# Local attention on one core: the inverse norms ahead of the rotation sum on GpSimd, the cosine product later on VectorE, the feed-forward part in 12 slots of 16

## What is computed

```
qkv = shift_tokens(x) @ Wqkv                        # 16 heads of 64
q = l2norm(q) * qs;  k = l2norm(k) * ksc
q = q * cos * scale + rotate_half(q) * sin * scale
k = k * cos / scale + rotate_half(k) * sin / scale
out = local_attention(q, k, v)                      # windows of 32, each sees itself and the one before
x = x + out @ Wo
x = x + (a * gelu(gate)) @ W2 + b2                  # a, gate from layernorm(x) @ W1 + b1, inner width 341
```

## Time and profile before

| | |
|---|---|
| median of three runs | 5737.72 us (5737.62 to 5739.98) |
| the profiled execution's own time | 5798.86 us |
| its span | 5797.1 us |
| TensorE matmuls busy | 5247.6 us, 91% |
| VectorE busy | 4111.8 us, 71% |
| ScalarE busy | 3595.0 us, 62% |
| GpSimd busy | 3474.3 us, 60% |
| mean granted TensorE clock | 0.927 of full speed |

### The profile page before, as it was taken

The page is one execution under the profiler, slowest core; times in us unless marked ns, Lnnn a source line. Parts: engine busy times, 40 slices in busy tenths (PEclk is TensorE's granted clock), DMA queues, the critical chain, the costliest instruction groups (busy, mean ns, idle before and its releaser), DMA issues. The chain is left out here.

```text
span 5797.1 us, 142985 instructions
## 1 busy us (share of the span) xinstructions
PE 5247.6 (91%) x46548; PEld 3130.0 (54%) x46548; DVE 4111.8 (71%) x8327; ACT 3595.0 (62%) x10714; POOL 3474.3 (60%) x3696
## 2 busy tenths in 40 slices
PE   7999999999999985899999999899999999999997
PEld 4666566565666652333433433566656666565664
DVE  5888888888888862344434443688888888888885
ACT  4887778777787760022222222587777877777775
POOL 6888778777877751000000000788777777787784
PEclk8999999999999995588977897899999999999998
DMA  2121121212112111000000000212121121211211
GB/s 71 45 58 45 50 50 42 55 45 52 48 42 55 45 31 21 0 1 1 1 1 1 1 1 1 70 44 57 44 53 48 42 56 44 52 49 45 52 45 31
DMA packets 297778, 216.57 MB, mean 37 GB/s; under 512 B 83197, under 2 KB 294681, under 8 KB 296217
## 3 DMA queue, kind: packets, MB, share of 16 engines
q1 hardware_dynamic: 296984, 206.69, 14.1%
HBM read 41.87 MB, written 1.05 MB: 7 GB/s over the span
## 5 line engine op out<-in xcount | busy, mean ns | idle before, releaser
L742 ACT ACTIVATE prob<-ps,nmx,inv 128x96 f32<-128x96 f32 x3072 | 1284.1, 430 | 309.6 <-PE ps L673 266.1
L545 POOL TENSOR_TENSOR rot<-t 128x512 f32<-128x512 f32 x768 | 1026.8, 1337 | 714.8 <-DVE t L820 661.7
L549 POOL TENSOR_TENSOR inv<-ssm,neg_half 128x8 f32<-128x8 f32 x768 | 1415.7, 1843 | 0.0
L828 DVE TENSOR_TENSOR prob<-prob,rec 128x384 f32<-128x384 f32 x768 | 912.8, 1189 | 26.2
L627 PE MATMUL ps<-w_qkv,xs 128*128 128x512 f32 x1536 | 877.4, 654 | 59.0 <-DVE t L820 39.5
L1287 ACT ACTIVATE ptl<-ps_l 128x1024 f32<-128x1024 f32 (+1 forms) x288 | 281.1, 976 | 967.3 <-PE ps_l L1162 733.4
L836 DVE TENSOR_REDUCE mx<-ps 128x4 f32<-128x384 f32 x768 | 424.1, 552 | 377.5 <-PE ps L654 374.8
L673 PE MATMUL ps<-ident,prob 128*96 128x128 f32 x3072 | 475.7, 278 | 214.1 <-DVE prob L828 213.2
L742 ACT ACTIVATION_READ_ACCUMULATOR prob<-ps,nmx,inv 128x1 f32 x3072 | 622.8, 203 | 0.0
L820 DVE TENSOR_TENSOR t<-ps,tab_s 128x256 f32<-128x256 f32 x1536 | 572.0, 414 | 0.0
L735 ACT COPY vt<-ps 128x256 f32<-128x256 f32 x768 | 285.3, 371 | 435.2 <-PE ps L665 424.2
(11 more groups left out here) (201 smaller groups left out, 8635.7 us busy)
## 6 DMA issues: line engine op xcount, KB each, us to landing
vs<-vt SPq DMA_DIRECT2D x768, 96.0 KB, 2.2
vs<-vt SPq DMA_DIRECT2D x768, 64.0 KB, 2.0
vs<-vt SPq DMA_DIRECT2D x768, 32.0 KB, 1.8
xs<-x_a SPq DMA_DIRECT2D x384, 32.0 KB, 1.9
w_qkv<-in_L_ffn_Wqkv SPq DMA_DIRECT2D x48, 256.0 KB, 3.8
w_qkv<-in_L_ffn_Wqkv SPq DMA_DIRECT2D x48, 128.0 KB, 3.4
w_o<-in_L_ffn_Wo SPq DMA_DIRECT2D x12, 512.0 KB, 4.1
w<-in_L_ffn_W SPq DMA_DIRECT2D x12, 341.0 KB
```

Source lines behind the costliest of these rows:

```text
L545: nc.gpsimd.tensor_tensor(rot[:, n % 4], t1[:, n % 2], t2[:, n % 2], ALU.add).then_inc(z["rotated"], 1)
L549: nc.gpsimd.tensor_tensor(inv[:, n % 4], ssm[:, n % 2], neg_half[:, 0:2 * HU], ALU.pow).then_inc(z["inv_ready"], 1)
L742: e = nc.scalar.activation(prob[:, n % 2, h, :], scores[:, h % 2, h // 2, :], ACT.Exp, scale=inv[:, n % 4, h:h + 1], bias=nmx[:, n % 2, h: ...
L828: nc.vector.tensor_tensor(prob[:, n % 2], prob[:, n % 2], rec[:, n % 2].unsqueeze(2).to_broadcast([P, HU, SKEYS]), ALU.mult).then_inc(z["w ...
```

## The change

The phases of the feed-forward part are drawn together from slots 0 to 15 into slots 0 to 11, and four slots of each sixteen have none. On TensorE the feed-forward product moves ahead of the turn of `prob`; on VectorE the feed-forward step moves ahead of the sum of squares; on ScalarE square, gate copy and shift move behind the copy of the output. On GpSimd the power (`inv`) and the carrying of keys move ahead of the rotation sum, and the sum is done in two halves, keys first, each with a semaphore of its own. On VectorE the sine products come first, and the cosine product moves behind `nmx`. TensorE's query-key product waits for `t1_ready` instead of `t2_ready`. SP loads the feed-forward weights four slots earlier. What is computed stays the same.

```diff
--- before.py
+++ after.py
@@ -64,14 +64,15 @@
 
 
 
-PHASE = dict(shift=0, mean=1, centre=1, square=2, var=2, eps=2, rstd=3, diag=3, spread=4, scale=4,
-             gate=(5, 7, 8), gate_copy=(6, 8, 9), gelu=11, up=(11, 12, 13), prod=(11, 12, 13), down=15, add=15)
+PHASE = dict(shift=0, mean=1, centre=1, square=1, var=2, eps=2, rstd=2, diag=2, spread=3, scale=3,
+             gate=(4, 5, 6), gate_copy=(4, 5, 6), gelu=7, up=(7, 8, 9), prod=(7, 8, 9), down=11, add=11)
+
 
 
 SEMAPHORES = (
     "const_in consts_ready x_in wq_in_0 wq_in_1 wq_in_2 wq_in_3 wv_in_0 wv_in_1 wv_in_2 wv_in_3 wo_in sc_in wf_in"
 
-    " xs_in_0 xs_in_1 tab_ready qk_ready squared summed clamped inv_ready t1_ready t2_ready rotated k_normed"
+    " xs_in_0 xs_in_1 tab_ready qk_ready squared summed clamped inv_ready t1_ready t2_ready rotated_k rotated_q k_normed"
     " tr_ready tr_read s_ready k_carried maxed negated exped recip_ready weighted pt_ready pt_read v_ready v_read"
     " v_strips_0 v_strips_1 v_strips_2 v_strips_3"
     " o_ready ot_read y_ready x_b_ready"
@@ -406,7 +407,7 @@
 
         def feed(j, part):
             g, p = divmod(j - LAG_Y, 16)
-            return (p, g - 1) if not (part == "first" and g < 1) else (None, None)
+            return (p, g - 1) if p <= 11 and not (part == "first" and g < 1) else (None, None)
 
         def group_no(L, g):
             return (L + L0) * G + g
@@ -420,7 +421,7 @@
             with eng.Fori(1, DEPTH) as L:
                 for j in range(UNITS):
                     slot(L, j, "steady")
-            for j in range(UNITS, UNITS + LAG_Y + 16):
+            for j in range(UNITS, UNITS + LAG_Y + 12):
                 slot(DEPTH - 1, j, "last")
 
         block = st.enter_context(nc.Block())
@@ -478,7 +479,7 @@
                         if j == LAG_Y:
                             sp.wait_ge(z["y_ready"], (L + L0) * TILES)
                             output_weights(L)
-                        if j == LAG_Y + 15:
+                        if j == LAG_Y + 11:
                             sp.wait_ge(z["x_a_ready"], (L + L0) * G + 1)
                             feed_forward_weights(L)
                     if j == UNITS - 6:
@@ -538,24 +539,28 @@
                     nc.gpsimd.tensor_tensor(f_rstd[:, :], f_var[:, :], neg_half[:, 0:GT // P], ALU.pow).then_inc(z["pow_ready"], 1)
                 if live(LAG_R):
                     n = (j - LAG_R) % 8
-                    pool.wait_ge(z["t1_ready"], done(LAG_R))
-                    pool.wait_ge(z["t2_ready"], 2 * done(LAG_R))
-                    if had(LAG_R, 4):
-                        pool.wait_ge(z["tr_ready"], done(LAG_R, 4))
-                    nc.gpsimd.tensor_tensor(rot[:, n % 4], t1[:, n % 2], t2[:, n % 2], ALU.add).then_inc(z["rotated"], 1)
                     pool.wait_ge(z["clamped"], done(LAG_R))
                     if had(LAG_R, 4):
                         pool.wait_ge(z["exped"], done(LAG_R, 4))
                     nc.gpsimd.tensor_tensor(inv[:, n % 4], ssm[:, n % 2], neg_half[:, 0:2 * HU], ALU.pow).then_inc(z["inv_ready"], 1)
-                    pool.wait_ge(z["rotated"], done(LAG_R))
-                    pool.wait_ge(z["inv_ready"], done(LAG_R))
-                    kh = rot[:, n % 4, QK // 2:QK].rearrange("p (h d) -> p h d", d=DH)
-                    nc.gpsimd.tensor_tensor(kh, kh, inv[:, n % 4, HU:2 * HU].unsqueeze(2).to_broadcast([P, HU, DH]), ALU.mult).then_inc(z["k_normed"], 1)
                 if live(LAG_S + 1):
                     m = (j - LAG_S - 1) % 8
                     pool.wait_ge(z["s_ready"], done(LAG_S + 1))
                     nc.gpsimd.tensor_tensor(qkt[:, (m + UT) % 8, 2:4, 0:WIN], qkt[:, m, 2:4, P:KEYS],
                                             carry_f[:, 0:1].unsqueeze(2).to_broadcast([P, 2, WIN]), ALU.mult).then_inc(z["k_carried"], 1)
+                if live(LAG_R):
+                    n = (j - LAG_R) % 8
+                    half = {"q": slice(0, QK // 2), "k": slice(QK // 2, QK)}
+                    pool.wait_ge(z["t1_ready"], done(LAG_R))
+                    pool.wait_ge(z["t2_ready"], 2 * done(LAG_R))
+                    if had(LAG_R, 4):
+                        pool.wait_ge(z["tr_ready"], done(LAG_R, 4))
+                    for w in ("k", "q"):
+                        nc.gpsimd.tensor_tensor(rot[:, n % 4, half[w]], t1[:, n % 2, half[w]], t2[:, n % 2, half[w]], ALU.add).then_inc(z["rotated_" + w], 1)
+                    pool.wait_ge(z["rotated_k"], done(LAG_R))
+                    pool.wait_ge(z["inv_ready"], done(LAG_R))
+                    kh = rot[:, n % 4, half["k"]].rearrange("p (h d) -> p h d", d=DH)
+                    nc.gpsimd.tensor_tensor(kh, kh, inv[:, n % 4, HU:2 * HU].unsqueeze(2).to_broadcast([P, HU, DH]), ALU.mult).then_inc(z["k_normed"], 1)
                 if live(0) and j % UT == 1:
                     if had(0, 2):
                         pool.wait_ge(z["t2_ready"], 2 * done(0, 2))
@@ -623,7 +628,7 @@
                         pe.wait_ge(z[f"xs_in_{j // UT % 2}"], tokens_in(L, j // UT))
                     if had(0, 2):
                         pe.wait_ge(z["squared"], done(0, 2))
-                        pe.wait_ge(z["t2_ready"], 2 * done(0, 2))
+                        pe.wait_ge(z["t1_ready"], done(0, 2))
                     pe.matmul(ps[:, j % 2, :], xs[:, j // UT % 2, :], w_qkv[:, 0:2, u * 256:(u + 1) * 256],
                               start=True, stop=True).then_inc(z["qk_ready"], 1)
                 if live(LAG_Y) and (j - LAG_Y) % UT == UT - 1:
@@ -664,6 +669,8 @@
                         pe.wait_ge(z["ot_read"], done(LAG_O, 1))
                     pe.matmul(ps[:, 6, 0:256], xs[:, n // UT, :], w_qkv[:, 2, (n % UT) * 256:(n % UT + 1) * 256],
                               start=True, stop=True).then_inc(z["v_ready"], 1)
+                if p is not None:
+                    feed_forward(L, p, g)
                 if live(LAG_P):
                     n = (j - LAG_P) % 8
                     pe.wait_ge(z["weighted"], done(LAG_P))
@@ -672,8 +679,6 @@
                     for h in range(HU):
                         mm = pe.transpose(ps[0:SKEYS, 5, h * P:(h + 1) * P], prob[:, n % 2, h, :], ident[:, :])
                     mm.then_inc(z["pt_ready"], 1)
-                if p is not None:
-                    feed_forward(L, p, g)
                 if live(LAG_T):
                     pe.wait_ge(z["k_normed"], done(LAG_T))
                     if had(LAG_T, 1):
@@ -713,17 +718,6 @@
                     if had(0, 2):
                         act.wait_ge(z["summed"], done(0, 2))
                     nc.scalar.activation(sq[:, j % 2], ps[:, j % 2, :], ACT.Square).then_inc(z["squared"], 1)
-                if p == PHASE["shift"]:
-                    act.wait_ge(z["x_b_ready"], group_no(L, g) * 4 + 4)
-                    nc.scalar.copy(f_src[0:64, :], x_b[0:64, 1 + g % G * GT:1 + (g % G + 1) * GT]).then_inc(z["sh_lo"], 1)
-                if p == PHASE["square"]:
-                    act.wait_ge(z["ln_centred"], norm_no(L, g) + 1)
-                    nc.scalar.activation(f_sq[:, :], f_xc[:, :], ACT.Square).then_inc(z["ln_squared"], 1)
-                if p in PHASE["gate_copy"]:
-                    m = PHASE["gate_copy"].index(p)
-                    w = CH[m][1]
-                    act.wait_ge(z["gate_up"], group_no(L, g) * 3 + m + 1)
-                    nc.scalar.activation(f_gate[0:w, m, :], ff[0:w], ACT.Identity, bias=vec[0:w, 6 + m:7 + m]).then_inc(z["gate_read"], 1)
                 if p == PHASE["gelu"]:
                     act.wait_ge(z["gate_read"], group_no(L, g) * 3 + 3)
                     nc.scalar.activation(f_gate[:, :, :], f_gate[:, :, :], ACT.Gelu).then_inc(z["gelu_ready"], 1)
@@ -753,6 +747,17 @@
                     n = (j - LAG_O) % 8
                     act.wait_ge(z["o_ready"], done(LAG_O))
                     nc.scalar.copy(ots[:, n].rearrange("p a t -> p (a t)"), ps[:, 6, HV]).then_inc(z["ot_read"], 1)
+                if p == PHASE["square"]:
+                    act.wait_ge(z["ln_centred"], norm_no(L, g) + 1)
+                    nc.scalar.activation(f_sq[:, :], f_xc[:, :], ACT.Square).then_inc(z["ln_squared"], 1)
+                if p in PHASE["gate_copy"]:
+                    m = PHASE["gate_copy"].index(p)
+                    w = CH[m][1]
+                    act.wait_ge(z["gate_up"], group_no(L, g) * 3 + m + 1)
+                    nc.scalar.activation(f_gate[0:w, m, :], ff[0:w], ACT.Identity, bias=vec[0:w, 6 + m:7 + m]).then_inc(z["gate_read"], 1)
+                if p == PHASE["shift"]:
+                    act.wait_ge(z["x_b_ready"], group_no(L, g) * 4 + 4)
+                    nc.scalar.copy(f_src[0:64, :], x_b[0:64, 1 + g % G * GT:1 + (g % G + 1) * GT]).then_inc(z["sh_lo"], 1)
                 if live(LAG_P):
                     n = (j - LAG_P) % 8
                     act.wait_ge(z["pt_ready"], done(LAG_P))
@@ -811,9 +816,7 @@
                     dve.wait_ge(z["squared"], done(LAG_R))
```

(9 more changed lines are left out.)

## The result

The changed kernel takes 5480.87 us in the median of four runs (5473.91 to 5501.35), the kernel before 5738.85 us in the median of its four (5737.62 to 5834.20). The ratio of the mean times is 0.9518 (95% interval 0.9464 to 0.9572), that of the medians 0.955. The nearest of the cases was rival A.

What follows compares the result with a forecast made beforehand. TensorE, busy 80.60 of 86.81 us a looped group, waits for VectorE's weighting, lengthened by GpSimd's sum. Groups of 82.0 us save (86.8 - 82.0) x 40 = 192, x 0.9895 = 190; 5737.7 - 190 = 5548 us, range 5483 to 5645.

Steps and rivals of the forecast that it cites:

- rival A: TensorE's floor: all waits but gelu's rest vanish, 80.6 us a group, 5483 us; chance 0.07.
- (1): GpSimd's power and key carry ahead of the sum: 12.8 us mostly leave VectorE, looped group falls 4.6 us.
- rival E: GpSimd's power holds off VectorE's weighting for its whole 1.64 us: slower, about 6310 us; chance 0.03.
- (2): New meetings of sum halves and key norm with VectorE's instructions: its group 73 us at most, no cost under TensorE's 80.2.
- rival B: Clamp, weighting and `nmx` each meet a half or the key norm: 0.9 us a slot, 84.4 a group, 5643 us; chance 0.11.
- (3): Two halves on GpSimd instead of one sum: 0 to 0.18 us more a slot, hidden by TensorE's 80 us.
- (4): TensorE's query-key product waits for the later cosine product: 0.5 us of slack, so no cost.
- rival D: Query-key product waits for the cosine product: TensorE loses 0.5 us a slot, 90 a group, 5911 us; chance 0.06.
- (5): Feed-forward in slots 0 to 11 and its new places: taken as nothing, with 0.9 us lost at the gelu as now.
- the gelu's 0.9: ScalarE's gelu slot: 7.9 us where TensorE needs 6.5; with half a us of slack, 0.9 us lost.
- 80.2 busy + 0.9 gelu + 0.9 other waits = 82.0: Looped group's forecast in us: TensorE's busy time, the gelu's loss, and other waits taken from the first layer.
- the ratio 0.9895: Factor carrying savings from the profiled scale to unprofiled runs: 192 us saved becomes 190.

Runs made afterwards that it cites:

- P: Kernel before with only power and key carry moved ahead of the whole sum on GpSimd: 5694.5 us, ratio 0.9832, looped group 84.28 us.
- P, H and T: Changed kernel with the feed-forward part put back to 16 slots and old places: 5589.2 us, ratio 0.9625, looped group 81.66 us.
- H: Rotation sum in two halves; added to P on the kernel before: 5600.6 us; undone in the changed kernel: 5517.3 us, ratio 0.9543.
- T: Cosine product late, behind `nmx`; added to P on the kernel before: 5554.1 us; undone in the changed kernel: 5570.0 us, ratio 0.9616.

## Why the prediction fell short

(1) Right in kind. The power doesn't hold the weighting off (0.56 us inside a power), and rival E is out. I priced the 12.8 us of lengthened weighting as VectorE's load. For half of the slots of the kernel before the rows bear that out. What the prediction lacked is that order sets a second limit, the loops that close over the exponentials: through GpSimd with P alone, through reciprocal, weighting, products, maxima and `nmx` with the weighting ahead (shorter weighting, less load, slower kernel). How much of the 5.2 us of P, H and T is load and how much is such a loop avoided isn't shown.

(2) The clamp takes 376 ns, 0.2 a slot over its bare 0.17, where I allowed 0.4 in the mean; in the four free slots, for which I took 0.5, it is 0 to 0.4 longer. The weighting meets the key norm in part of the slots (begun 0.15 us into one, it takes 0.87) and stays at 729. VectorE's group is 66.6 us, well under the 73 allowed, and rival B is out.

(3) Nearly right: the halves take 753 ns each, 1.51 for both where 1.25 to 1.45 was forecast; GpSimd's group is 69.78 us for the 69 forecast. Left out was what they bring: 2.0 us a group without T, 0.7 with T, 0.5 in the changed kernel.

(4) Right: no wait at the query-key product within the looped group; rival D is out.

(5) Wrong: "nothing" for the feed-forward part. It gives 1.76 us a group once P, H and T are there, 1.54 of it by the places, and 7.8 us a looped layer. The forecast of its own chain (eps, power, diagonal) held to 0.1 us, and so, nearly, did the gelu's 0.9 with 0.78.

The step that failed is the sum, "80.2 busy + 0.9 gelu + 0.9 other waits = 82.0". Measured: 79.1 + 0.8 + 0, so two terms were too large. The other waits went with (5): with P, H and T alone TensorE still waits 1.1 us a group for the weighting, with the new places none. And 80.2 was no floor: TensorE's busy time for the same instructions is 81.42 us in the slow order, 80.60 before, 79.12 after, 79.05 in 16 slots with new places. It tends to be longer where the group is longer, though not in step (80.79 with P alone, whose group is 84.28). I took it for work, and with it rival A's 80.6, from which the lower end of the range comes, lay above the measured group. By the steps between starts the work would have been 16 x 3.83 + 4 x 1.82 + 8 x 0.86 and some 3.4 for variance and down, 78.9 us, and the group's 79.9 is that sum and the gelu's wait to 0.2. The changed kernel's own steps from one query-key product to the next agree: 3.83 us in a free slot, 4.69 with a product, 5.65 with an output projection, 6.47 with both.

On the looped groups I forecast 192 us and 278 came. The medians show 258, but the four runs of before alone spread over 97 us, and later sets of the same kernel had medians of 5791.4 (13 runs) and 5773.4 us (7 runs), so the whole time gives the gain to some 50 us only. For the same reason the ratio 0.9895, between the profiled run and the others, was no scale for the stacks; it cost the forecast 2 us. And by the prediction's own sum groups of 81 us give 5508 us, or 5501 with the first layers, not 5490.

## What to carry to other kernels

Before weighing a meeting of two engines by its length, ask whether it lies on a loop between engines: taking 0.44 us a slot off `nmx`, between maxima and exponentials, gave 1.9 us a group, although the clamp, beside the exponentials, grew by 0.5 us a slot in exchange. Such a loop can run through an engine that seems to have time to spare, by a wait for a free buffer. Moving a blocked instruction earlier can close another loop; see in the new order what each engine waits for. Take an engine's floor from the starts of its instructions in a stretch without waits, not from its busy time, which differed by 2.4 us between orders of the same instructions. And hold whole layers against each other beside groups, since part of a gain can lie at the boundary.

## What the hardware showed

The latent part has the same instructions in every kernel here, and VectorE and ScalarE are as busy to 0.5 us. Yet it took 1370 us in the trace of before, 1347 in that of after, and in two of the experiments (12 slots in old places; the feed-forward part alone) this:

```profile
2261.29:3569.04 1307.75, 1189.36 (x6532) 499.25 (x6532) 542.86 (x681) 309.16 (x335) 119.83 (x144) 0.83 0.00 1
```

```profile
2249.62:3666.95 1417.33, 1303.86 (x6532) 534.17 (x6532) 543.12 (x681) 309.15 (x335) 119.83 (x144) 0.75 0.00 1
```

The granted clock of TensorE is 0.83 of full speed in the mean of the one and 0.75 in that of the other. Within such a part it changes between two levels: in the changed kernel it is 0.50 from 2500 to 2502 us and 1.00 from 2510 to 2512. So the shares of the two differ from run to run; the stacks, at 1.00 in every group compared, are steady. These 110 us are 2% of the kernel, and a smaller effect can't be read from single times. What sets the shares wasn't tried.

A power of eight elements takes 1.64 us, and 1.96 where a weighting was still under way at its start; why was not tried. A two-input instruction of VectorE that starts inside it is not slowed: in the changed kernel 184 weightings, 0.56 us each, and 456 `nmx`, 0.17 at most.
